# A graph propagation kernel: source tiles grouped by three instead of two, first halves in steps of four chunks, the running total on GpSimd

## The reference

```python
def _propagate(all_emb, rows, cols, vals):
    acc = all_emb
    x = all_emb
    for _ in range(N_LAYERS):                       # 3
        x = segment_sum(vals[:, None] * x[cols], rows, num_segments=N_NODES)
        acc = acc + x
    return acc / (N_LAYERS + 1)
...
rating = users_emb @ items_emb.T
rating = rating + bias_user[users] + bias_item.T
return sigmoid(rating)
```

## Time and profile before

| | |
|---|---|
| runs | 5386.48 us median of 3 (5386.25 to 5393.11) |
| the profiled execution | 5386.6 us, span in the trace 5384.8 us |
| mean granted TensorE clock | 0.86 |
| preparation | 0 to 1444.3 us |
| first halves | 842.9, 840.0, 842.1 us |
| second halves | 378.9, 378.5, 383.7 us |
| ratings | 183.8 us |
| busy | DVE 89%, PE 62%, ACT 45%, POOL 45% |

### The profile page before, as it was taken

One profiled execution on the slowest core, in us unless ns is written; L12 is line 12 of the kernel. 1 busy time (PEld: TensorE's weight loads), 2 busy tenths in 40 slices (PEclk: granted clock), 3 DMA queues, 4 the chain that ended last, 5 costly groups with the idle time before them and its releaser, 6 DMA issues.

```text
span 5384.8 us, 195868 instructions
## 1 busy us (share of the span) xinstructions
PE 3361.2 (62%) x71235; PEld 2864.2 (53%) x71473; DVE 4793.2 (89%) x7569; ACT 2443.1 (45%) x4368; POOL 2415.1 (45%) x2161
## 2 busy tenths in 40 slices
PE   5600021111288888777678888867768888867767
PEld 4500011110277777666567777756657777766652
DVE  9989999999999999877799999967789999977778
ACT  0035555553366666500156666620046666640027
POOL 0038763330177777700067777730037777760000
PEclk9955555555699999999999999989989999989989
DMA  9960000300188778799968878889968777879999
GB/s 329 415 260 0 0 0 3 5 0 0 64 248 253 248 246 247 234 321 328 279 213 251 248 256 249 249 276 328 328 191 255 249 245 246 249 241 328 328 281 357
DMA packets 840272, 1191.20 MB, mean 221 GB/s; under 512 B 150792, under 2 KB 667583, under 8 KB 839825
## 3 DMA queue, kind: packets, MB, share of 16 engines
q1 hardware_dynamic: 716032, 816.66, 53.2%
q0 software_dynamic: 123872, 372.78, 18.0%
q10 hardware_dynamic: 304, 1.00, 0.1%
HBM read 638.35 MB, written 551.90 MB: 221 GB/s over the span
## 4 chain that ended last, share of the span: by engine, by line
DVE 28%; DMA 28%; issue 20%; POOL 9%; PE 6%; ACT 5%; SPq 1%; DVEq 1%; POOLq 0%; another core or an unknown queue 0%; ACTq 0%
DMA ring<-posts 15%; DMA posts<-ring 9%; POOL posts L775 9%; DVE store L1064 6%; PE psum L1501 4%; DVE total L861 3%; ACT new L695 3%; DVE store L1042 3%; DVE ring L1271 3%; DVE store L1043 2%; DMA out<-new 2%; DVE new L1243 2%; DVE ring L1256 2%; DVE ring L1295 2%; DMA ring<-lanes_d 1%
## 5 line engine op out<-in xcount | busy, mean ns | idle before, releaser
L775 POOL DMA_INDIRECT posts<-ring x1884 | 1852.6, 983 | 1740.6 <-DVE ring L1256 1154.0
L1477 PE MATMUL psum<-store,ring 128*128 x45216 | 2086.2, 197 | 497.9 <-DVE ring L1271 461.6
L1477 PEld LDWEIGHTS psum<-store,ring 128*128 128x128 bf16 x45216 | 1815.1, 100 | 769.2 <-issue 591.4
L695 ACT ACTIVATE new<-new 128x512 bf16<-128x512 uint8 x1884 | 1067.8, 614 | 0.0
L1271 DVE TENSOR_SCALAR ring<-ring,lane_f 128x1024 bf16<-128x1024 bf16 x1884 | 959.7, 551 | 23.4 <-DMA ring<-lanes_d 22.0
L1295 DVE TENSOR_TENSOR ring<-ring,wide_lane 128x1024 bf16<-128x1024 bf16 x948 | 612.9, 688 | 300.1 <-ACT ring L705 300.1
L1256 DVE TENSOR_TENSOR ring<-new 128x1024 bf16<-128x1024 bf16 x942 | 652.2, 692 | 93.8 <-ACT new L695 63.3
L693 ACT ACTIVATE ring<-new 128x512 bf16<-128x512 bf16 x942 | 585.9, 622 | 310.3 <-DVE new L1243 308.2
L750 POOL TENSOR_TENSOR ring<-store 128x1024 f32<-128x1024 f32 x157 | 369.6, 2354 | 660.6 <-DVE store L982 306.3
L1243 DVE TENSOR_TENSOR new<-psum,vals_m 128x512 f32<-128x512 f32 x942 | 644.1, 684 | 6.1 <-PE psum L1477 4.0
L1501 PE MATMUL psum<-ring 128*128 128x64 bf16 x11520 | 387.4, 193 | 188.7 <-DVE ring L1295 180.9
(11 more groups left out here) (228 smaller groups left out, 2666.1 us busy)
## 6 DMA issues: line engine op xcount, KB each, us to landing
ring<-lanes_d SPq DMA_DIRECT2D x471, 512.0 KB
ring<-posts SPq DMA_DIRECT2D x240, 772.0 KB, 6.7
store<-posts SPq DMA_DIRECT2D x234, 772.0 KB, 6.7
posts<-store SPq DMA_DIRECT2D x2, 30880.0 KB, 166.7
posts<-store SPq DMA_DIRECT2D x2, 30108.0 KB, 128.5
out<-new SPq DMA_DIRECT2D x96, 500.0 KB, 8.4
posts<-ring POOLq DMA_INDIRECT x1884
store<-L_rec_bias_item SPq DMA_DIRECT2D x1, 3125.0 KB, 13.8
```

The source lines that it names most:

```text
L695: last = nc.scalar.activation(digits[s][:, k, :], scaled_byte[s][k], ACT.Copy, scale=scale)
L775: pool.indirect_dma_start(out=posts[:, :], out_offset=bass.IndirectOffsetOnAxis(ap=dring[:, h, c:c + 1], axis=0), in_=msg[:, n, :], in_off ...
L1477: last = pe.matmul(psum[:, d % 4, (n % 2 * BLOCK + b) * F:(n % 2 * BLOCK + b + 1) * F], of, xflat[:, bass.ds(at_d[c] * F + (k * XT + x * F ...
```

## The change

A super becomes three tiles, 384 columns, and there are 49 supers (147 = 3 x 49). Fewer supers need fewer dummies: 580 chunks in place of 628. A chunk now takes three one-hots and 4 x 3 x 3 = 36 matmuls; lanes run to 383 and are stored less 192. The first half goes in steps of four chunks: each DVE and ACT instruction covers twice the columns, there are four PSUM slots of two banks, and the message ring is refilled in quarters of four chunks. One-hots, digits and powers move from `ring` to `new` and `scaled` moves the other way, so `idx` and the remainders of the cast (`rest`) no longer share memory, and SP may load lanes before the cast is over. POOL adds `new` to `total` at a layer's start, before its scatters; DVE waits for it before the first one-hots. Fewer dummies also make the second half shorter: 152 steps in place of 158.

```diff
-SUPERS = -(-TILES // 2)
+WAYS = 3
+SUPERS = -(-TILES // WAYS)
...
-SENT_ROWS = [16 * (8 * BODIES + REST), 16 * 8 * BODIES]
-DUOS = CHUNKS // 2
+SENT_ROWS = [16 * (4 * BODIES + REST)] + 3 * [16 * 4 * BODIES]
+QUADS = CHUNKS // 4
...
@@ SP
-                sp.wait_ge(s_x3, (layer + 1) * SPLITS)
+                if layer:
+                    sp.wait_ge(s_unit, layer * ITERS + GOTS)
...
-                        sp.wait_ge(s_hots, i * 8 + (layer * DUOS + h * 4 + b * 2 + 2))
+                        sp.wait_ge(s_hots, i * 4 + (layer * QUADS + d + 3))
...
@@ ACT
-                def take_apart(i, first, pairs=8):
-                    for d in range(pairs):
+                def take_apart(i, first, quads=4):
+                    for d in range(quads):
                         s = d % 2
-                        if d % 4 == 0:
-                            refill(i, d // 4, first, min(8, 2 * pairs - 2 * d))
-                        act.wait_ge(s_scaled, i * 8 + (layer * DUOS + d + 5))
-                        nc.scalar.activation(msg_parts[:, 0, 4 * d:4 * d + 4, :], scaled_high[s], ACT.Copy).then_inc(s_high, 1)
+                        refill(i, d, first)
+                        act.wait_ge(s_scaled, i * 4 + (layer * QUADS + d + 5))
+                        nc.scalar.activation(msg_parts[:, 0, 8 * d:8 * d + 8, :], scaled_high[s], ACT.Copy).then_inc(s_high, 1)
...
@@ POOL
+                for q in range(SPLITS):
+                    a, b = q * SPLIT, (q + 1) * SPLIT
+                    if layer == 0:
+                        nc.gpsimd.tensor_copy(total3[:, a:b, :], new3[:, a:b, :]).then_inc(s_taken, 1)
+                    else:
+                        nc.gpsimd.tensor_tensor(total3[:, a:b, :], total3[:, a:b, :], new3[:, a:b, :], ALU.add).then_inc(s_taken, 1)
...
@@ DVE, preparation
-            link(nc.vector.tensor_scalar(bits_b, cols_i, 8, None, ALU.logical_shift_right))
+            link(nc.vector.tensor_scalar(bits_b, cols_i, 7, None, ALU.logical_shift_right))
+            link(nc.vector.tensor_scalar(bits_b, bits_b, float(THIRD), None, ALU.mult))
+            link(nc.vector.tensor_scalar(bits_b, bits_b, THIRD_BITS, None, ALU.logical_shift_right))
...
@@ DVE, first half
-                def send(i, first, pairs=8):
-                    for d in range(pairs):
-                        h, j = d // 4, d % 4
-                        dve.wait_ge(s_sent, i * 8 + (layer * DUOS + d + 1))
+                def send(i, first, quads=4):
+                    for d in range(quads):
+                        h, b = d // 2, d % 2
+                        dve.wait_ge(s_sent, i * 4 + (layer * QUADS + d + 1))
                         if not (first and d < 2):
-                            if first and d == 2:
-                                dve.wait_ge(s_taken, layer * SPLITS + 2)
-                            scale(i, (d + 6) % 8, d - 2)
...
-                        for k in range(2):
-                            last = nc.vector.tensor_scalar(hot[d % 2][:, k, :], idx[j // 2][:, j % 2 * 2 * CHUNK:(j % 2 + 1) * 2 * CHUNK],
-                                                           lane_f[:, k:k + 1], None, ALU.is_equal)
+                            scale(i, (d + 2) % 4, d - 2)
+                        dve.wait_ge(s_idx[b], i * 32 + (layer * HALF_LOADS[b] + h + 1) * 16)
+                        for k in range(WAYS):
+                            last = nc.vector.tensor_scalar(hot[b][:, k, :], idx[b], lane_f[:, 1 + k:2 + k], None, ALU.is_equal)
                         last.then_inc(s_hots, 1)
                         if not (first and d < 3):
-                            low_parts(i, (d + 5) % 8, d - 3)
-                        if first and d < SPLITS:
-                            take(layer, d)
+                            low_parts(i, (d + 1) % 4, d - 3)
+
+                dve.wait_ge(s_taken, (layer + 1) * SPLITS)
...
@@ PE
-                        d, c = n // 2, n % 4
+                        d, c = n // 4, n % 4
                         if c == 0:
                             at_d = supers(i, n)
-                        if n % 2 == 0:
-                            pe.wait_ge(s_hots, i * 8 + (layer * DUOS + d + 5))
-                            pe.wait_ge(s_scaled, i * 8 + (layer * DUOS + d + 1))
+                            pe.wait_ge(s_hots, i * 4 + (layer * QUADS + d + 5))
+                            pe.wait_ge(s_scaled, i * 4 + (layer * QUADS + d + 1))
                         for b in range(BLOCK):
-                            for k in range(2):
+                            for k in range(WAYS):
```

More of the change, by code:

```diff
@@ L32 @@
 SENTINEL = -float(1 << 100)
-SUPERS = -(-TILES // 2)
+WAYS = 3
+SUPERS = -(-TILES // WAYS)
+assert SUPERS * WAYS == TILES
+THIRD, THIRD_BITS = 171, 9
+assert all(t * THIRD >> THIRD_BITS == t // WAYS for t in range(TILES))
+LANE_ZERO = WAYS * P // 2
 BLOCK = 4
@@ L228, in build @@
         idx = [ring[:, b * 1024:(b + 1) * 1024].bitcast(BF16) for b in range(2)]
-        hot = [ring[:, 2048 + s * 1024:3072 + s * 1024].bitcast(BF16).rearrange("p (k e) -> p k e", k=2) for s in range(2)]
+        hot = [new[:, s * WAYS * 1024:(s + 1) * WAYS * 1024].bitcast(BF16).rearrange("p (k e) -> p k e", k=WAYS) for s in range(2)]
         msg = ring[:, 4096:4096 + 16 * ROW].rearrange("p (s w) -> p s w", w=ROW)
@@ L357, in build @@
         s_high = sem("s_high")
-        s_scat = [sem(f"s_scat{h}") for h in range(2)]
+        s_scat = [sem(f"s_scat{h}") for h in range(4)]
         s_got = [sem(f"s_got{s}") for s in range(GOTS)]
@@ L696, in take_apart @@
                         last.then_inc(s_digits, 1)
+                act.wait_ge(s_x3, (layer + 1) * SPLITS)
                 take_apart(0, True)
@@ L1193, in _ @@
             link(nc.vector.tensor_scalar(super_f, super_f, float(SUPERS - 1), None, ALU.min))
[L1194 to L1195 removed]
+            nc.vector.tensor_scalar(super_d[:, :], super_f, float(WAYS * PARTS), None, ALU.mult).then_inc(s_decoded, 1)
             dve.wait_ge(s_uoff, 16)
@@ L1317, in _ @@
                 add(0, 0, tiles_at(0, 1)[0])
-                with dve.Fori(0, (ITERS - 2) // GOTS) as i:
+                with dve.Fori(0, ADD_BODIES) as i:
                     at_t = tiles_at(i * GOTS + 1, GOTS)
@@ L1322, in _ @@
                         add(i * 2, 1 + g, at_t[g])
-                add(ITERS // 2, -1, tiles_at(ITERS - 1, 1)[0])
+                for s in range(ADD_BODIES * GOTS + 1, ITERS - 1):
+                    prepare(0, s + 1, (s + 1) % GOTS)
+                    add(0, s, tiles_at(s, 1)[0])
+                add(0, ITERS - 1, tiles_at(ITERS - 1, 1)[0])
             dve.wait_ge(s_add, LAYERS * ITERS + 2)
@@ L1461, in supers @@
                         super_d[0:1, bass.ds(i * 16 + n, 4)], engines=(mybir.EngineType.PE,), min_val=0,
-                        max_val=(SUPERS - 1) * 2 * PARTS, skip_runtime_bounds_check_because="the chip clamps each above")[1]
+                        max_val=(SUPERS - 1) * WAYS * PARTS, skip_runtime_bounds_check_because="the chip clamps each above")[1]
                 def sums(i, chunks=16):
                     for n in range(chunks):
-                        d, c = n // 2, n % 4
+                        d, c = n // 4, n % 4
                         if c == 0:
                             at_d = supers(i, n)
-                        if n % 2 == 0:
-                            pe.wait_ge(s_hots, i * 8 + (layer * DUOS + d + 5))
-                            pe.wait_ge(s_scaled, i * 8 + (layer * DUOS + d + 1))
+                            pe.wait_ge(s_hots, i * 4 + (layer * QUADS + d + 5))
+                            pe.wait_ge(s_scaled, i * 4 + (layer * QUADS + d + 1))
                         for b in range(BLOCK):
-                            for k in range(2):
-                                of = hot[d % 2][:, k, n % 2 * CHUNK + b * P:n % 2 * CHUNK + (b + 1) * P]
+                            for k in range(WAYS):
+                                of = hot[d % 2][:, k, c * CHUNK + b * P:c * CHUNK + (b + 1) * P]
                                 for x in range(PARTS):
-                                    last = pe.matmul(psum[:, d % 4, (n % 2 * BLOCK + b) * F:(n % 2 * BLOCK + b + 1) * F], of,
+                                    last = pe.matmul(psum[:, 2 * d + c // 2, (c % 2 * BLOCK + b) * F:(c % 2 * BLOCK + b + 1) * F], of,
                                                      xflat[:, bass.ds(at_d[c] * F + (k * XT + x * F), F)],
-                                                     start=(k == 0 and x == 0), stop=(k == 1 and x == PARTS - 1), skip_group_check=True)
-                        if n % 2 == 1:
+                                                     start=(k == 0 and x == 0), stop=(k == WAYS - 1 and x == PARTS - 1), skip_group_check=True)
+                        if c == 3:
                             last.then_inc(s_sent, 1)
@@ L1485, in _ @@
                 sums(BODIES, chunks=REST)
-                pe.wait_ge(s_scaled, (layer + 1) * DUOS + 4)
```

(1 more changed line is left out.)

120 lines of the change are left out of this document (58 added, 62 removed).

## The result

The changed kernel takes 5736.8 us (median of four runs, 5735.4 to 5738.7) against 5387.1 (four runs, 5386.3 to 5393.1): ratio 1.0647, interval 1.0628 to 1.0665. The forecast was 5735. The profiled execution has a span of 5736.7 us, 351.9 more than before.

The account below looks back on a forecast made before the run. PE's address operations were to bound the first half at 6.65 us per four chunks, against 5.29. Per layer 135.8 - 2.9 + 1.3 - 14.4 = 119.8 us, three times 359.4, less 11.5, on 5386.6: 5735 us, range 5430 to 5850.

Parts of the forecast that it names:

- first to last matmul: First half of each layer: from 829.9 to 963.7 us, +135.8 us against the mean of 827.9.
- last matmul to last scatter: End of each layer's first half: from 11.9 to 13.2 us, +1.3 us.
- second halves, from the last scatter on: Second half of each layer: 152 steps of 2.40 us in place of 158, -14.4 us.
- preparation and first lead: Preparation: fewer rows to zero, -11.5 us; first layer's start: first one-hots no longer wait for lanes, -2.9 us.
- What bounds PE: First half: nine address operations 0.124 us apart and 17 matmuls allowed to wait make 6.65 us per four chunks.
- hand-over: First half, behind each chunk's ninth address operation: 0.39 us until the next chunk's first address operation.
- 32 matmuls with their weight loads: First half, rival: PE's queue holds all 28 matmuls, a step is 5.98 us, total 5444 us; chance 0.12.
- The load: First half, PE's offset load per four chunks: taken as 0.62 us, between bounds of 0.33 and 0.96.
- The lead: Layer start, before the first matmul: lane wait goes, POOL's additions end just inside the cast, -2.9 us a layer.
- the refill wait: First half: ACT's 201 us of waiting for landed rows go away, but into PE's time.
- rival (c): First half: granted clock falls to 1.2 GHz for a third of the steps, total 5990 us; chance 0.05.
- (b): First half, rival: POOL and DVE keep the pace at 5.29 us a step, total 5144 us; chance 0.05.

Follow-up runs that it names:

- e7: Changed kernel with a chunk's blocks in two halves, two matmuls behind each address operation and 20 behind the ninth: 5400.5 us.
- e2: Changed kernel with the running total back on VectorE in three pieces, POOL adding nothing: 5697.5 us, ratio 1.0591.
- e6: Kernel before the change with the four blocks innermost around the matmul, nothing else changed: 5368.9 us, ratio 0.9996.
- e9: Changed kernel with blocks innermost, running total on VectorE, and every fourth POOL transfer left out: 5242.6 us.
- e8: Changed kernel with blocks innermost, running total on VectorE, and only two of three DVE comparisons: 5352.2 us.
- e5: Changed kernel with the four blocks innermost around the matmul and the running total on VectorE in three pieces: 5283.9 us, ratio 0.9835.
- e1: Changed kernel with only the matmul order changed, the four blocks innermost: 5316.3 us, ratio 0.9885.

## Why the prediction was right

The time came out within 2 us, but that is luck: two errors of some 30 us nearly cancel. In us, three layers together, from the profiled executions:

| term | predicted | measured |
|---|---|---|
| first to last matmul | +407.4 | +379.8 |
| leads of layers two and three | -5.8 | +30.1 |
| last matmul to last scatter | +3.9 | +3.9 |
| second halves, from the last scatter on | -43.2 | -46.0 |
| preparation and first lead | -14.4 | -15.9 |
| sum | +347.9 | +351.9 |

**What bounds PE** was right in mechanism, and nearly in number. The changed kernel's address operations stand 0.124 us apart, 17 matmuls wait behind the run, and the hand-over is 0.42 us for a predicted 0.39. That this sequence sets the pace is shown by the exchange of loops, which leaves every matmul and address operation in place and takes 147 us from a first half; that DVE doesn't, by the run with two comparisons. In e7 the same 17 held behind a run of 20. The Trainium skill ("Advanced Engine Details and Errata", section Engine Queue Depths) gives TensorE's queue 64 places; 32 matmuls with their weight loads is my estimate from that figure, and by it the time would have been 5444 us. The trace does not agree: no step in three layers had more than 17 matmuls waiting there, and the measurement decides.

**The load** was the term mis-sized. I took 0.62 us from a range of 0.33 to 0.96. Line L1471, 1470 to 2380 us:

```profile
L1471 PEldq TENSOR_LOAD <-super_d x138: 331/335/602, 1470.0 to 2375.4; - x138
```

The median is the lower end, 0.335, and the mean of all 435 is 0.357. Before, 414 of 471 were longer than 0.36 us, and 405 of these began while POOL was in a transfer instruction and ended 0.3 us after it (median). I had expected the same mixture; in the changed kernel only 46 are longer, though most of the short ones, 328 of 389, also begin during a transfer. What makes one long stays open. From the last address operation to the next step's first it takes 1.23 us on average, predicted 1.40; three hand-overs of 0.428 on average, for 0.39, give 0.10 back. A step is 6.57 to 6.62, not 6.65.

**The lead** is the step that failed: "-2.9 us" was +15 in layers two and three. That the wait for lanes would go was right, and so was the order of events. What failed is "POOL's seven additions [...] take 21.6 us [...], just inside the cast; if VectorE's traffic slows them by a quarter, 4 us show". I asked what DVE does to POOL and not what POOL does to DVE. The lead before (columns of the earlier trace rows):

```profile
2677.30:2705.70 28.40, 0.00 (x1) 0.01 (x1) 22.25 (x17) 17.86 (x16) 0.00 (x0) 0.55 0.10 36
```

After the change it is 43.5 us. Timeline from the layer's end at 2778.4:

```profile
2778.49 28.77 POOL L786 TENSOR_TENSOR total<-total,new 128x1344 f32<-128x1344 f32 x7 [367.10 <-DVE new L1314]
2779.90 7.32 DVE L1235 TENSOR_TENSOR ring<-new,store 128x1344 f32<-128x1344 f32 x2 [1.49 <-ACT store L669]
...
2787.14 4.37 DVE L1241 TENSOR_TENSOR store<-ring,store 128x1344 bf16<-128x1344 f32 x1
...
2804.31 4.37 DVE L1241 TENSOR_TENSOR store<-ring,store 128x1344 bf16<-128x1344 f32 x1
...
2808.79 1.56 DVE L1235 TENSOR_TENSOR ring<-new,store 128x1344 f32<-128x1344 f32 x1
...
2819.59 4.07 DVE L1281 TENSOR_SCALAR new<-ring,lane_f 128x2048 bf16<-128x2048 bf16 x6
```

While POOL adds, until 2807.3, DVE finishes seven subtractions in 28.8 us, one for each addition: the first takes 3.0 us, the others 4.2 to 4.4; from then on each takes 1.55 again. The seven lose 28.8 - 7 x 1.55 = 17.9 us, and 43.5 - 17.9 = 25.6 is the lead that I had predicted (28.5 - 2.9). The run with the total on DVE shows the cause: no additions on POOL, 1.55 us for each subtraction, a lead of 29.2 with 3.4 of them for DVE's own first piece. The Trainium skill ("SBUF — State Buffer", section Who interferes with whom) says that a VectorE instruction with two SBUF inputs and a GpSimd instruction that reads SBUF exclude each other for the whole instruction; the trace agrees: POOL's first addition, begun 1.4 us ahead of any subtraction, takes 3.0 us, and from the second on each takes 4.3, about its own time and a subtraction's 1.55.

**The other terms** held: the refill wait went into PE's time, DVE waits for PE at each step (its instructions there take 4.9 us, priced at 5.7 to 6.3), and second halves are 364.5 us. The granted clock is 0.98 in the first half of layer one, so rival (c) had no part; (b) would have needed PE to keep up at 5.29.

The row of the preparation and the first lead hides two more errors that cancel. The zeroing of `posts` takes 302.9 us in place of 314.0, counted to the first small transfer, as forecast; but it also begins 5.9 us earlier, at 43.0, which no term had. So that transfer moves 17 us earlier, at 345.9, while DVE's and POOL's waits stay at 14.6 and 21.5 us. Against this the first lead grew from 29.0 us, first cast to first matmul, to 33.0, where I had -2.9: POOL copies `new` beside the same subtractions. In e2, without that copy, it is 27.6.

## What to carry to other kernels

Where matmuls take addresses from registers, count address operations and look at what stands behind each: a run behind the last one can't cover the next ones once it exceeds what may wait (17 matmuls here), while the same matmuls spread evenly behind the operations cover all of them. When two engines are to work side by side, price both directions: the work that was moved, and the work that it was moved beside. And price an order of loops on the engine that the change makes the limit; in the kernel before, the same exchange was worth nothing.

## What the runs showed of the hardware that I had not expected

POOL's transfer instruction is not of one length: its length goes with where in a DVE instruction it begins. Two timelines, first of the run with blocks inside, then of the run without the third tile's matmuls:

```profile
1907.48 1.22 DVE L1269 TENSOR_TENSOR ring<-new 128x2048 bf16<-128x2048 bf16 x1
...
1908.26 1.29 POOL L794 DMA_INDIRECT posts<-ring  x1 [0.30 <-issue]
...
1909.85 0.97 POOL L794 DMA_INDIRECT posts<-ring  x1 [0.30 <-issue]
```

```profile
1905.24 2.08 DVE L1281 TENSOR_SCALAR new<-ring,lane_f 128x2048 bf16<-128x2048 bf16 x3
1905.33 1.49 POOL L794 DMA_INDIRECT posts<-ring  x1 [0.30 <-issue]
```

Begun 0.8 us into the last multiplication it takes 1.29 us, begun 0.1 us into the comparisons 1.49, and begun beside the scaling, which reads PSUM, 0.97. I sorted all transfer instructions by that distance in all the runs but e2, e6 and e9. A start 0.075 to 0.2 us into the comparisons gives a median of 1.39 to 1.49 in each layer where it occurs often; an earlier one gives 0.96 to 0.97; 0.6 to 0.8 us into the four-chunk multiplication it is 1.29, and with nothing beside it 0.96 to 0.97. This fits with what fewer comparisons did in e8: in its first two layers 192 instructions begin 0.075 to 0.2 us into the comparisons, in its third only 15, and 46 earlier than that; in e5 none do. So the same work has two phases, one of them slower. That the phase makes the time is read from the traces and was not tried by an edit, and what picks it I have not tried to settle.

PE's load of offsets, where it is long, ends with POOL's transfer instruction in e1, e5 and e7, though not in e8 and e9: of the 208 loads in e5 over 0.36 us that began during one, the median ended 0.025 us ahead of its end, with 0.015 us between the tenth and the ninetieth percentile. In the kernel before, it was 0.3 us after it. What holds the load was not tried.
